# Front stage of a two-layer byte model: when a group's projections take their turn beside the next group's four tiles

## The reference

```python
h = _L0_tok_ref(x, emb_2, emb_3, emb_4, proj_w, proj_b)   # n-gram hash -> three gathered rows -> 384x128 projection
h = h + _L0_attn_ref(_layernorm(h), W_Q, W_K, W_V, W_G, W_O, gn_weight, gn_bias)
#   inside: Q = _xpos(X @ W_Q), K = _xpos(X @ W_K), V = X @ W_V, G = X @ W_G
#   scores = Q K^T per head, softmax * decay, @ V, group norm, silu(G) * Y, @ W_O
h = h + _L0_ffn_ref(...)      # mixture of 8 experts
h = h + _L1_attn_ref(...)     # 8 heads of width 128
h = h + _L1_ffn_ref(...)      # latent attention, most of the time
```

## Time and profile before

| | us |
|---|---|
| median of 3 runs | 3011.66 |
| lowest and highest | 3009.15, 3014.8 |
| the profiled execution, its own time | 3014.42 |
| its span, first to last instruction | 3012.3 |

### The profile page before, as it was taken

How to read it: one execution, slowest core, us unless ns; L and a number is a source line. 1 busy time by engine, 2 the same in 40 slices (tenths; PEclk the granted TensorE clock), 3 DMA queues, 4 the chain that set the end, 5 groups by cost and what they waited for, 6 DMA issues and landing times.

```text
span 3012.3 us, 44556 instructions
## 1 busy us (share of the span) xinstructions
PE 2763.5 (92%) x14620; PEld 2255.7 (75%) x14652; DVE 2306.6 (77%) x4019; ACT 1750.5 (58%) x3388; POOL 2067.8 (69%) x1504
## 2 busy tenths in 40 slices
PE   4698786979999999689999999999999999999996
PEld 3476564867888888568888888887777787788875
DVE  3599887446667676588888888888888888888884
ACT  2598785435666565255666566655555555556653
POOL 7499784107777777257777777777676777777773
PEclk8799998989999999799999999999999999999997
DMA  2011000000000000111111011111110010101100
GB/s 84 22 26 25 22 22 29 1 29 1 1 1 1 1 1 1 65 35 36 42 35 46 33 35 46 35 34 42 35 46 33 33 35 32 53 33 35 46 19 8
DMA packets 44691, 87.00 MB, mean 29 GB/s; under 512 B 10676, under 2 KB 24780, under 8 KB 43824
## 3 DMA queue, kind: packets, MB, share of 16 engines
q1 hardware_dynamic: 42928, 81.00, 8.3%
q0 software_dynamic: 1536, 3.15, 0.4%
HBM read 64.44 MB, written 1.05 MB: 22 GB/s over the span
## 4 chain that ended last, share of the span: by engine, by line
PE 48%; DVE 5%; issue 2%; POOL 1%; ACT 1%; POOLq 0%; ACTq 0%; DVEq 0%
PE lat_ps_h L2239 17%; PE lat_ps_z L2250 10%; PE lat_ps_s L2189 8%; PE lat_ps_t L2218 7%; PE lat_ps_s L2205 3%; PE lat_ps_s L2196 2%; DVE latm_attT L1918 1%; DVE latm_sc L1903 1%; DVE latm_top L1898 1%; DVE latm_tot L1910 1%; POOL lat_zz L1866 1%; DVE lat_wq_sum L1923 0%; PE lat_ps_s L2272 0%; DVE lat_share L1937 0%; ACT lat_zsq L2096 0%
## 5 line engine op out<-in xcount | busy, mean ns | idle before, releaser
L1853 POOL TENSOR_TENSOR latm_att<-latm_sc,latm_tot 128x500 f32<-128x500 f32 (+1 forms) x416 | 421.6, 1013 | 432.7 <-DVE latm_tot L1912 421.8
L2239 PE MATMUL lat_ps_h<-latm_attT,lat_share 125*128 125x512 f32 (+1 forms) x2472 | 682.6, 408 | 22.0 <-DVE latm_attT L1918 18.8
L1866 POOL TENSOR_TENSOR lat_zz<-lat_zz,lat_zsq 128x512 f32<-128x512 f32 x508 | 658.5, 1296 | 23.2 <-ACT lat_zsq L2096 15.8
L2089 ACT CAST latm_attT<-lat_ps_t 125x512 fp32r<-125x512 f32 (+1 forms) x512 | 301.7, 589 | 618.1 <-PE lat_ps_t L2218 618.1
L2239 PEld LDWEIGHTS lat_ps_h<-latm_attT,lat_share 125*128 125x128 f32 (+1 forms) x2472 | 460.2, 189 | 150.2 <-DVE latm_attT L1918 45.4
L2250 PE MATMUL lat_ps_z<-latm_attT,lat_vc 100*128 100x512 f32 x1536 | 483.8, 423 | 0.2 <-ACT lat_zsq L2096 0.2
L1061 POOL TENSOR_SCALAR mha_probs<-mha_probs,mha_inv 128x1024 f32<-128x1024 f32 x128 | 364.8, 2850 | 112.2 <-DVE mha_inv L1282 112.2
L1918 DVE TENSOR_TENSOR latm_attT<-lat_ps_t,latm_attT 125x512 fp32r<-125x512 f32 (+1 forms) x512 | 347.9, 680 | 102.7 <-ACT latm_attT L2089 102.3
L2189 PE MATMUL lat_ps_s<-lat_wk,lat_xr 128*128 128x500 f32 (+1 forms) x1248 | 350.3, 389 | 11.6 <-PEq L97 4.8
L371 POOL TENSOR_TENSOR ret_probs<-ret_probs,ret_shared 128x1024 f32<-128x1024 f32 x128 | 306.5, 2429 | 48.3 <-ACT ret_probs L583 48.3
L2218 PEld LDWEIGHTS lat_ps_t<-ident,latm_att 128*125 128x125 f32 (+1 forms) x2048 | 283.4, 174 | 64.0 <-POOL latm_att L1853 16.7
(11 more groups left out here) (365 smaller groups left out, 4786.9 us busy)
## 6 DMA issues: line engine op xcount, KB each, us to landing
lat_w_in<-in_w_fives SPq DMA_DIRECT2D x52, 640.0 KB, 4.2
lat_wq_in<-in_wq_fives SPq DMA_DIRECT2D x52, 320.0 KB, 2.9
lat_share<-lat_share SPq DMA_DIRECT2D x200, 50.0 KB
ret_qk_head<-ret_qk_parts SPq DMA_DIRECT2D x256, 32.0 KB, 2.0
moe_w<-in_W SPq DMA_DIRECT2D x2, 1024.0 KB, 5.5
ret_xpos<-in_xpos_q SPq DMA_DIRECT2D x1, 1024.0 KB, 6.0
ret_xpos<-in_xpos_k SPq DMA_DIRECT2D x1, 1024.0 KB, 8.8
latw_wkv<-in_Wkv SPq DMA_DIRECT2D x1, 1024.0 KB
```

The lines of the kernel that those rows point to most:

```text
L1853: nc.gpsimd.tensor_tensor(att[:, k % SLOTS].rearrange("p (j l) -> p j l", j=QH)[:, 0:n, 0:L], sc[:, u, 0:n * L].rearrange("p (j l) -> p j ...
L1866: nc.gpsimd.tensor_tensor(dst, dst, zsq[:, n % 2], ALU.add).then_inc(s["zz_added"], 1)
L2239: mm = e.matmul(ps_h[:, f, c, :], share[0:w, q % 2, w_part, cols], attT[0:w, n % 2, a_part], start=(n % NS in (0, QH) and (a_part, w_part) ...
```

## The change

On three engines the order of the same instructions changes; no instruction, wait or buffer is added or removed. In every round g the four tiles and the norm of group g are written first, and the projections of group g-1, with all their casts and rests, behind them.

```diff
--- before.py
+++ after.py
@@ -425,9 +425,9 @@
                     turn_rows(t)
                     if t % 4 > 0:
                         embed(t - 1)
-                    if g >= 1 and t % 4 == 2:
-                        project(g - 1)
                 embed(4 * g + 3)
+                if g >= 1:
+                    project(g - 1)
             project(NG - 1)
             e.wait_ge(s["proj_used"], START + 2 * NG)
             e.wait_ge(s["vg_used"], START + 2 * NG)
@@ -565,12 +565,10 @@
             for g in range(NG):
                 for t in range(4 * g, 4 * g + 4):
                     embed(t)
-                    if g >= 1 and t % 4 == 2:
-                        take_group(g - 1)
-                if g >= 1:
-                    take_part(g - 1, 1)
                 spread(g)
                 if g >= 1:
+                    take_group(g - 1)
+                    take_part(g - 1, 1)
                     take_part(g - 1, 2)
             take_group(NG - 1)
             take_part(NG - 1, 1)
@@ -695,15 +693,14 @@
             e.wait_ge(proj_in, 32)
             hide(0)
             for g in range(NG):
-                if g >= 1:
-                    turn_qk(g - 1)
-                    rest(g - 1, 0)
                 if 4 * g + 3 in edge:
                     hide(4 * g + 3)
                 normal(g)
                 if 4 * g + 4 in edge:
                     hide(4 * g + 4)
                 if g >= 1:
+                    turn_qk(g - 1)
+                    rest(g - 1, 0)
                     rest(g - 1, 1)
             turn_qk(NG - 1)
             e.wait_ge(consts_in, 80)
```

## The result

| | before, us | after, us |
|---|---|---|
| median of 10 runs each | 3009.94 | 3018.21 |
| lowest to highest | 3006.79 to 3014.80 | 3013.35 to 3022.81 |
| the profiled execution, its own time | 3014.42 | 3021.36 |
| its span | 3012.3 | 3019.2 |

The ratio is 1.0024, with a 95% interval of 1.0016 to 1.0032: the change makes the kernel slower by 7.2 us (4.8 to 9.6). The ratio is an estimate of its own and not the quotient of the two medians, which lie 8.3 us apart; where the text gives a difference in us between kernels, it is worked out from the ratio unless it says otherwise. A second measurement of the same kernel, on another occasion, gave 1.0029 (1.0018 to 1.0040). The forecast was 1.8 us less, and a time longer by over 0.2% had been given 6 in 100. The median lies above the stated range.

What follows compares the result with a forecast made beforehand. The first stage was taken as bound by a chain hopping between engines: 9.5 us gained in front grows to 12.3 at group 3's norm, 10.5 is given back, leaving 1.8 us less, 3009.9 us; range 3005 to 3014.5.

Steps and rivals of the forecast that it cites:

- The front: First stage's start: tile 7's mask 9.5 us earlier, at 39.8, and group 1's norm at 43.7.
- From the norm's start to the copy to `xT`: First part of each round: ACT stands behind the norm's root, 4.1 us.
- one surcharge: DVE's second rests of group 1 beside POOL's splitting of values: 0.25 us added once, upper bound 0.5.
- item 2: From the copy to `xT` to the next group's first tile copy, through ACT's casts and DVE's rests: 13.15 us.
- item 3: From first tile copy to next norm, PE transposing and projecting tiles: 6.45 us, bound 7.2 if the clock stays low.
- rival of tiles at 1.2 GHz throughout: PE's four tiles per round stay at the low clock: +1.5 us over both rounds, net -0.3 us; 20%.
- the hold: Follow-up theory, not in the prediction: DVE's TENSOR_SCALAR in group 2's norm waits while POOL's memset runs, 6.36 us.
- The clock rival: Projections stay at 1.2 GHz to their end after PE's idle time: 1.0 us three times, net +1.2 us; 10%.
- The rest of the kernel: Everything from the first scores on: the same 2890.9 us before and after, within the runs' scatter.
- theory E: Follow-up theory, not in the prediction: the 2 us left above the kernel before is work elsewhere, with every execution's front alike.

Runs made afterwards that it cites:

- a_tt: Changed kernel with DVE's scaling of the norm's sums written as TENSOR_TENSOR instead of TENSOR_SCALAR; 3011.73 us, ratio 1.0008 to the kernel before.
- a_late: Changed kernel with POOL's memset issued behind the wait for group 1's values; 3013.40 us, ratio 1.0007 to the kernel before.
- a_split: Changed kernel with POOL's memset cut into eight pieces in the same place; 3013.80 us, ratio 1.0010 to the kernel before.
- b_same: The kernel before, unchanged, measured against itself; 3050.39 us, ratio 1.0002.
- b_late: The kernel before, in its old order, with POOL's memset issued behind the wait for group 1's values; 3014.73 us, ratio 1.0017 to the kernel before.
- after_again: The changed kernel without any edit, measured a second time; 3021.55 us, ratio 1.0029 to the kernel before.
- a_warm_both2: Changed kernel with TENSOR_TENSOR scaling and four extra PE matmuls ahead of each projection and of groups 2 and 3's tiles; 2999.50 us, ratio 0.9962 to the kernel before.

## Why the prediction was wrong

**The front.** Right: the mask 9.3 us earlier, the norm of group 1 at 43.85, and that the gain is given back at the tail. The first tile copy of group 2 came at 61.11, as the sum had it (60.95) and no earlier than before (60.45); the norm of group 2 still began 9.6 us earlier than before (68.01 against 77.56), and that is what met the memset.

**"From the norm's start to the copy to `xT`", 4.1 us.** This is the step that failed. It took 3.96 us for groups 1 and 3, and 10.15 for group 2. I read it off one norm, group 1's, beside which POOL issued gathers, and applied it to one that had been moved to a time when POOL ran another instruction. The prediction placed group 2's norm at 67.4 and gave the last gather's start as 67.30; it never asked what POOL did behind it. The memset of 6.94 us stood there in the timeline before, and a hint did too: group 2's TENSOR_SCALAR, of which 0.17 us was the rule, took 0.45 at 79.01, beside POOL's small instructions. The prediction allowed for POOL slowing DVE only in "one surcharge" of 0.25 us, for the rests. Of its rivals none was this one.

**The other terms of the sum**, which came to 108.6 for the copy to `xT` of group 3, against 115.93: norm of group 1 +0.15; item 1, "From the norm's start to the copy to `xT`", -0.14 twice and +6.05; item 2 13.30, 13.88 and 13.13 us, +0.6 over the three with the surcharge counted; item 3 6.90 and 6.80 us, +0.8. Together 7.3. (The parts given for item 2 add up to 13.1, not 13.15; that is within rounding.) Item 3 lay between 6.45 and the bound of 7.2: the clock rose, but later than in group 0. It was granted at 0.50 from 61.7 to 66 us and at 0.67 from 66 to 68, and the last twelve passes of the stretch took 2.28 us, where group 0's took 1.89. The rival of tiles at 1.2 GHz throughout, priced at 1.5 us, thus came about half way. Without the hold the new order was worth 0.1 to 0.8 us at the first score by the three profiles (0.7 in a_tt), not 1.8, and the ratios of a_late, a_tt and a_split (+2.1 to +3.0 us, two of the three intervals reaching 0) don't show even that. From -0.7 to +2.4 (a_tt) are 3.1 us; the clock, as counted above, would explain 1.5 of them. Whether the rest, 1.6 us, is real stays open: b_same's own interval is 0.0009 wide to either side, and a_tt's median lies only 0.6 us above that of the kernel before.

**The clock rival** was half right. I had the projections staying at 1.2 GHz to their end, at 1.0 us a round. They did rise (in the third or fourth product of each round), but later than before, and the second rotation waited 0.33, 0.48 and 0.11 us for it in the first three rounds: 0.9 us in place of 3.0. Item 2 took 0.86 us longer in the three rounds together, of which the surcharge had allowed for 0.25. Beyond that the loss was against the old order's occasional luck of being up from the first product, which one profile of before could not show.

**The rest of the kernel** took 2892.2 us against 2890.9; over all profiles it lies between 2887.5 and 2894.0, in the old order between 2888.5 and 2894.0 and in the new one without extra matmuls between 2889.0 and 2892.7. This is scatter, as forecast, and nothing in it speaks for theory E.

## What to carry to other kernels

When a change moves an instruction to another time, list what every other engine runs at that time, and not only whom it waits for. Here a DVE tensor-scalar on four numbers a partition took up to 6.4 us beside a POOL memset of 6.9. In a stage with such a chain three remedies worked: cutting the memset in pieces, moving it, and another kind of DVE instruction; b_late shows that a memset can also be moved onto the next such instruction. Where PE stands idle for some microseconds in each turn of a latency-bound chain, extra matmuls in the gap can be worth more than a better order: here 11 us against none. They must be done when the operand arrives: in the last round they were not, and gained nothing.

## What the runs showed of the hardware

- A DVE TENSOR_SCALAR on 128x4 f32 waited for the end of a POOL MEMSET of 128x8192 (6.36, 6.35 and 4.16 us in after, after_again and b_late, to within 0.03 us of its end), though the two share no data; a TENSOR_TENSOR of the same size took 0.16 us beside it (a_tt). Nothing marks the time as a wait: it is counted as busy.
- TensorE after 4.2 us without work ran the next product at 1.2 GHz (2.07 us, in after), and after 0.3 us, behind extra matmuls, at 2.4 GHz (1.12 us, in a_warm_both2). After the same 0.77 us of idle time and the same work before it, it was at either level from one execution to the next (2.05 us at 66.23 in before, 1.10 us at 65.68 in b_late).
- In two sessions the kernel before ran in 3049 to 3050 us instead of 3010 to 3011, on other chips. In the profile of b_same the first score came 31.8 us later than in the first profile of the same kernel; ACT waited 29.9 us in three places and DVE 20.7 us in one for what the profile calls remote. The cause is open.
